# Decoder layer on one core: the softmax sums of attention go to PSUM, and VectorE reads them out before the next scores

## The reference, cut to what matters

```python
q = _rmsnorm(_apply_partial_rope(q, cos, sin), g_qnorm)          # 8 heads of 64
k = _rmsnorm(_apply_partial_rope(h @ w_k, cos, sin), g_knorm)    # one key head
v = h @ w_v
sc_raw = einsum('bhqd,bnd->bhqn', q, kc) * scale                 # two block means per sequence
pc = softmax(concatenate([where(safe, sc_raw, NEG), sink], -1))
scores_full = einsum('bhqd,bkd->bhqk', q, k) * scale
ps = softmax(where(tok_sel, scores_full, NEG))
pw = softmax(concatenate([where(sw, scores_full, NEG), sink], -1))
g = sigmoid(q @ w_gate + b_gate); g = g / clip(g.sum(-1), 1e-06)
mixed = g[0] * comp_out + g[1] * sel_out + g[2] * sw_out
return einsum(mixed, w_out_group) @ w_out
```

## Time and profile before

| | us |
|---|---|
| median of 3 runs | 609.47 |
| lowest and highest of them | 603.3 and 613.24 |
| the profiled execution | 608.82 |
| its span, first to last instruction | 607.0 |

### The profile page before, as it was taken

The page is one execution under the profiler, slowest core; times in us unless marked ns, Lnnn a source line. Parts: engine busy times, 40 slices in busy tenths (PEclk is TensorE's granted clock), DMA queues, the critical chain, the costliest instruction groups (busy, mean ns, idle before and its releaser), DMA issues.

```text
span 607.0 us, 17806 instructions
## 1 busy us (share of the span) xinstructions
PE 514.6 (85%) x5418; PEld 408.6 (67%) x5418; DVE 472.7 (78%) x1699; ACT 438.0 (72%) x1290; POOL 435.8 (72%) x445
## 2 busy tenths in 40 slices
PE   6689887768888886999999999845898999999961
PEld 3456665656665663677777777635797999999820
DVE  3789988879999788577888889964885777899612
ACT  3799999989999777887888777512654656667603
POOL 7688988778989679365555699887777765687622
PEclk9889999999999898899999999965998999999987
DMA  2246555564522221111111111114223232623152
GB/s 74 96 174 236 207 189 198 217 198 118 150 77 53 71 69 51 37 41 41 42 42 41 50 43 41 50 45 103 67 79 78 73 87 69 198 67 94 48 173 69
DMA packets 72785, 58.45 MB, mean 96 GB/s; under 512 B 23128, under 2 KB 66270, under 8 KB 70646
## 3 DMA queue, kind: packets, MB, share of 16 engines
q1 hardware_dynamic: 67510, 47.79, 26.7%
q0 software_dynamic: 4608, 8.47, 4.3%
q10 hardware_dynamic: 576, 1.05, 0.6%
HBM read 26.40 MB, written 31.92 MB: 96 GB/s over the span
## 4 chain that ended last, share of the span: by engine, by line
PE 30%; POOL 20%; issue 18%; SPq 11%; DVE 9%; ACT 8%; DMA 3%; DVEq 0%; POOLq 0%; ACTq 0%
POOL l_keys L1062 8%; PE ps L1468 7%; POOL disp_dram L813 6%; ACT l_weights L394 6%; SPq L277 6%; PE ps L1494 5%; POOL l_rs L1057 4%; PE ps L1474 2%; PE ps L1505 2%; PE ps L325 1%; PE ps L348 1%; PE ps L337 1%; POOL y_dram L1628 1%; PE ps L355 1%; PE ps L1445 1%
## 5 line engine op out<-in xcount | busy, mean ns | idle before, releaser
L1628 POOL DMA_INDIRECT y_dram<-l_keys,m_blk x80 | 83.2, 1040 | 37.1 <-issue 19.4
L394 ACT ACTIVATE l_weights<-ps,a_nb,a_rinv 128x64 f32<-128x64 f32 x256 | 99.5, 412 | 6.6 <-DVE a_nb L517 5.4
L813 POOL DMA_INDIRECT disp_dram<-l_R,x_pos x64 | 64.2, 1004 | 17.6 <-issue 17.3
L483 POOL TENSOR_TENSOR a_rinv<-a_ms,a_halfneg 128x10 f32<-128x10 f32 (+1 forms) x32 | 62.5, 1952 | 5.2 <-DVE a_ms L549 4.0
L1062 POOL TENSOR_TENSOR l_keys<-x_kT,l_table 128x1024 f32<-128x1024 f32 x32 | 60.9, 1903 | 3.4 <-PE ps L878 3.4
L1130 DVE TENSOR_REDUCE x_mx<-ps 128x16 f32<-128x1024 f32 x32 | 39.1, 1223 | 25.4 <-PE ps L878 25.3
L355 PE MATMUL ps<-l_R,l_shifted 128*128 128x512 f32 x64 | 37.5, 670 | 23.9 <-DVE l_R L523 20.8
L394 ACT ACTIVATION_READ_ACCUMULATOR l_weights<-ps,a_nb,a_rinv 128x1 f32 x256 | 54.7, 214 | 0.0
L449 POOL TENSOR_TENSOR l_R<-l_weights,a_pa 128x512 f32<-128x512 f32 x32 | 33.3, 1042 | 26.5 <-DVE a_pc L611 26.5
L1057 POOL TENSOR_TENSOR l_rs<-x_ve,l_halfneg 128x2 f32<-128x2 f32 x32 | 24.5, 765 | 36.0 <-DVE x_ve L1190 35.6
L1494 PE MATMUL ps<-l_table,l_keys 128*128 x320 | 43.6, 279 | 3.3 <-ACT l_keys L1579 3.3
(11 more groups left out here) (232 smaller groups left out, 1692.9 us busy)
## 6 DMA issues: line engine op xcount, KB each, us to landing
disp_dram<-l_R SPq DMA_DIRECT2D x16, 1040.0 KB
m_blk<-disp_dram SPq DMA_DIRECT2D x80, 65.0 KB
l_shifted<-in_xT SPq DMA_DIRECT2D x32, 64.0 KB, 2.1
l_W1h<-v_dram SPq DMA_DIRECT2D x128, 16.0 KB, 2.4
l_R<-in_x SPq DMA_DIRECT2D x32, 64.0 KB, 2.0
x_dram<-a_xo SPq DMA_DIRECT2D x32, 64.0 KB, 1.7
l_W1l<-in_w SPq DMA_DIRECT2D x4, 512.0 KB
x_xa<-x_dram SPq DMA_DIRECT2D x32, 64.0 KB, 1.8
```

Source lines behind the costliest of these rows:

```text
L394: last = nc.scalar.activation(E[:, e.u4, g, :], ps_Sh[:, g % 2, g // 2, 0:D], ACT.Exp, bias=nb[:, e.u2, g:g + 1], scale=rinv[:, e.u4, g:g ...
L483: G.tensor_tensor(rinv[:, b.u4, 0:w], ms[:, b.u2, 0:w], halfneg[:, 0:w], ALU.pow).then_inc(inv_rms, 1)
L813: nc.gpsimd.indirect_dma_start(out=disp[:, :], out_offset=bass.IndirectOffsetOnAxis(ap=pos[:, B, k_, j:j + 1], axis=0), in_=R[:, t, k_, :] ...
L1628: G_.indirect_dma_start(out=Y[:, :], out_offset=bass.IndirectOffsetOnAxis(ap=blk[:, (2 * q + j) % NB, P:P + 1].bitcast(I32), axis=0), in_= ...
```

## The change

The sums of the exponentials are no longer written to `den` in SBUF by ScalarE but to eight columns of PSUM (bank 4, columns 328 to 335, beside the maxima). VectorE copies them to `den` as its first instruction of the next slot and counts a new semaphore, `den_read`. The scores of the next tile on TensorE wait for `den_read` in place of `exped`, and L596 waits for `den_read` too (on its own engine).

```diff
-    ps_mx = ps[:, 4, 320:320 + H]
+    ps_mx, ps_den = ps[:, 4, 320:320 + H], ps[:, 4, 328:328 + H]
...
+    den_read = sem("den_read")
...
                 e.wait(pe, qT_copied)
                 e.wait(pe, k_means)
-                e.free(pe, exped, 1)
+                e.free(pe, den_read, 1)
...
                     last = nc.scalar.activation(E[:, e.u4, g, :], ps_Sh[:, g % 2, g // 2, 0:D], ACT.Exp,
                                                 bias=nb[:, e.u2, g:g + 1], scale=rinv[:, e.u4, g:g + 1],
-                                                accum_out=den[:, e.u2, g, 1:2])
+                                                accum_out=ps_den[:, g:g + 1])
                 last.then_inc(exped, 1)
...
         def slot(at):
             b, c, d, e, f, k, l = (Tile(at, m) for m in (1, 2, 3, 4, 5, 8, 9))
+            if f.live:
+                f.wait(dve, exped)
+                f.free(dve, mixing, 2)
+                V.tensor_copy(den[:, f.u2, :, 1], ps_den).then_inc(den_read, 1)
             if e.live:
                 e.wait(dve, scored)
...
                 n.add(V.tensor_reduce(den[:, f.u2, :, 0], ex[:, f.u2, :, 0:3], AX.X, ALU.add))
+                f.wait(dve, den_read)
                 n_den = n.add(V.tensor_tensor(den[:, f.u2, :, 2], den[:, f.u2, :, 1], ex[:, f.u2, :, 3], ALU.add))
```

## The result

The changed kernel takes 673.22 us (median of 4 runs, 671.65 to 676.76) against 609.62 us before (median of 4). The ratio on record is 1.108 with a 95% interval of 1.103 to 1.113 (the two medians alone give 1.104): slower. The forecast was 678 us within 650 to 702. The profiled execution has a span of 669.9 us, 62.9 more than before.

What follows compares the result with a forecast made beforehand. Bounds were taken to alternate: SyncE's queue during loads, nearly full VectorE and ScalarE in calm slots. 608.8 us + 49.3 for longer slots + 20.0 for half clock = 678 us, range 650 to 702.

Steps and rivals of the forecast that it cites:

- The ring: VectorE and TensorE per slot: copy, scores, maxima in a row, 8.1 us for 6.01, 44.8 us more over 25 slots.
- The second meeting, L348 and L523: VectorE's L523 waits for TensorE's L348, now measured from the copy; 2.72 us from mask matmul to L523, 0.7 to 0.8 idle.
- The clock: TensorE, idle 2.3 us a slot, falls to half clock: half of 1.48, 0.74 us a slot, 20.0 us over 27 slots.
- clock held: Rival: TensorE's clock stays up despite 2.3 us of idle time a slot; 658 us, chance 0.25.
- half clock in every slot: Rival: TensorE's clock falls in nearly every slot just as the scores start; 40.0 us, 698 us in all, chance 0.17.
- The early slots and the last two: Early four slots, paced by ScalarE: 0.5 us each, 2 us; last two intervals at 7.2 us each: 2.5 us more.
- The copy: From L611's start to the mask matmul: 0.08 us to the copy, copy 0.17, hand-over 0.15, extra waits 0.03.
- ScalarE: Sums written to PSUM: ScalarE's pace unchanged, 0 taken, with bounds of 0.7 us a slot either way.
- the sign that the reads would still start 0.38 us apart: In the changed kernel's profile, ScalarE's accumulator reads should keep their spacing of 0.38 us.
- that rival: ScalarE gains from PSUM: 0.09 us per accumulator read, 0.7 us a slot, 23 us over 32 slots, 586 us; chance 0.02.

Runs made afterwards that it cites:

- e1: Changed kernel with sums still in PSUM, but the copy behind the maxima and the scores waiting for the exponentials again: 608.79 us, ratio 0.998.
- e2: Changed kernel with sums in SBUF again and a same-size copy of the maxima to a scratch, which the scores wait for: 675.27 us, ratio 1.106.
- e4: Changed kernel with the copy moved into the slot where the exponentials end, ahead of VectorE's tail; scores still wait for it: 616.45 us, ratio 1.010.
- e5: Changed kernel with the four transposes of L310 done four times over to keep TensorE busy: 698.47 us against 652.34 before, ratio 1.074.
- e3: Against e2, the copy replaced by a bare semaphore count on VectorE, which the scores wait for: 661.19 us, ratio 1.084.
- e11: Kernel before, sums in SBUF, with GpSimd's sine product moved ahead of its two multiplications of the probabilities: ratio 1.007.
- e6: As e1, with the copy of the keys out of PSUM made by ScalarE instead of VectorE: ratio 0.999 to the kernel before.

## Why the prediction was right

Point by point, from the maxima of the first tile to those of the last, 193.0 us before and 279.1 - 21.6 = 257.5 after, 64.5 more where 69.3 were forecast:

- *The ring.* Right in place and size, 7.96 us for 8.08. e1 shows that the wait is its cause, e2 that the wait is enough, and e4 moves it by moving the copy. 25 slots at 7.96 us are 41 us more than before, 45 were forecast.
- *The second meeting, L348 and L523.* Right: 36.2 us of VectorE's waits are there, and e4, which hides the scores, is left with it alone (0.49 us in front of L524).
- *The clock.* The half that I took of 1.48 us, 18.5 us over the 25 slots (20.0 over 27), came out as 216 - 25 x 7.96 = 17 us, and e5 took 17.5 back. It comes from 13 of the 25 slots, at 1.3 us each in the mean. Slots with and without half clock took turns, as a mean of both bounds supposes. That rivals on either side, clock held and half clock in every slot, both fail is luck in part: the rows gave the two levels, not how often they would be met.
- *The early slots and the last two.* 1.0 us for 2, and 5.3 for 2.5, the latter as both met half clock.
- *The copy.* The sum 0.08 + 0.17 + 0.15 + 0.03 = 0.43 came out at 0.39, but in e3's expectation I counted the copy at its own 0.16 and forgot that the hand-over goes with it.
- *ScalarE.* Wrong: I took 0, since longer reads had kept the pace of 0.38 us. With PSUM as target of the accumulator read the pace is 0.34, and e2 brings 0.38 back, so the sign that the reads would still start 0.38 us apart failed. The failed step is the inference that the pace doesn't depend on where the write goes because it doesn't depend on how long it takes. The Trainium skill, "ScalarE: Activation LUTs", "Step-by-step: what each stage is for", had said that PSUM is the faster target. The measured pace agrees in kind, though here the ACTIVATE still writes SBUF and only the read of its accumulator goes to PSUM. It is worth 0.3 us a slot and not the 0.7 of that rival, and nothing in time that can be told from no change, as e1 has it too and runs at 0.998 (0.995 to 1.001).

What came behind the last maxima took 390.8 us against 396.0, and the first maxima came 3.6 us later. Over the traces of e1 to e4 the former goes from 392.6 to 396.7 us, over all of e1 to e11 the first maxima come at 18.8 to 21.4 us, in no order that follows the wait, and neither is explained here.

## What to carry to other kernels

Before a wait is handed from one engine to another, look where the new engine's queue stands at that time: here the condition was true 1.8 us before VectorE reached it, and the engine it freed was the one VectorE itself needed next, so an overlap of two engines became a row. The same copy, ahead of the last ten instructions of the slot and not behind them, costs 1% and not 11%. And a wait on the busiest engine's path is paid twice if it lets TensorE's clock fall.

## What the runs showed of the hardware

- ScalarE's exponentials with an accumulator output follow each other every 0.34 us when the sum goes to PSUM and every 0.38 us when it goes to SBUF, though the durations of their rows are no shorter (medians 453 and 226 ns in e1; 409 and 212 before).
- A semaphore count that VectorE's queue makes by itself was seen by TensorE before the instruction ahead of it had ended: the mask matmul starts 0.09 us behind the start of L616, which takes 0.17 us (e3). With a copy of 128x8 that makes the count it starts 0.30 us behind the copy's start.
- While GpSimd runs a product of two SBUF operands (0.81 us), a VectorE instruction that reads more than one operand from SBUF doesn't finish: L563 (one tensor, two columns of scalars), L561 and L604 (two tensors) stretched to 0.77, 0.72 and 0.58 us, each time until the product ended. L557, with 128x1 from SBUF as its only operand, keeps its 0.14 us inside the same product (e6). The Trainium skill, "SBUF — State Buffer", "Who interferes with whom", says that VectorE and GpSimd share a pair of ports, and that a VectorE instruction with two SBUF inputs contends with a GpSimd instruction that reads SBUF. The rows of L561 and L604 agree. VectorE can thus be held up by a product of GpSimd that it doesn't wait for.
